# Transformer layer on one core: the last products taken in another tile order, one balancing loop of fifty steps, and the final mixing shared by four engines

## The reference

```python
x = x + xattn(layernorm(x), ctx, mask, ...)      # 32 heads, 256 context rows
x = x + attn(layernorm(x), Wq, Wk, Wv, Wo)       # causal, rotary, 32 heads of 32
x = x + ffn(layernorm(x), ...)

def ffn(x, ...):                 # x in 4 streams of 256 columns
    x_norm = x * rsqrt(mean(x * x) + eps)
    H_res = sinkhorn_log(x_norm @ W_res.T + H_res_base)      # 4 x 4 a row
    H_pre = softmax(x_norm @ W_pre.T + H_pre_base)
    H_post = softmax(x_norm @ W_post.T + H_post_base)
    H_res = (1 - g) * I + g * H_res
    y = einsum('btnc,btn->btc', x_streams, H_pre) @ W_branch
    return einsum('btij,btjc->btic', H_res, x_streams) + einsum('btc,btn->btnc', y, H_post)
```

## Time and profile before

| | |
|---|---|
| median of 3 runs | 1153.63 us (1153.41 to 1156.05) |
| profiled execution, its own time | 1153.41 us |
| its span, first to last instruction | 1151.6 us |
| mean granted TensorE clock | 0.978 of full |
| busy, PE / DVE / ACT / POOL | 93% / 70% / 41% / 13% |
| chain that ended last, by engine | PE 82%, DVE 14%, ACT 2% |

### The profile page before, as it was taken

How to read it: one execution, slowest core, us unless ns; L and a number is a source line. 1 busy time by engine, 2 the same in 40 slices (tenths; PEclk the granted TensorE clock), 3 DMA queues, 4 the chain that set the end, 5 groups by cost and what they waited for, 6 DMA issues and landing times.

```text
span 1151.6 us, 17668 instructions
## 1 busy us (share of the span) xinstructions
PE 1071.5 (93%) x6392; PEld 899.6 (78%) x6392; DVE 808.7 (70%) x1843; ACT 477.0 (41%) x989; POOL 154.7 (13%) x162
## 2 busy tenths in 40 slices
PE   5999999999999999999999999999999999895565
PEld 3888888888888887888888887888888778784444
DVE  6744447567768868776678876675547799836998
ACT  4523324354454446544544455432223334313334
POOL 0000000333223222332332220000001000000000
PEclk9999999999999999999999999999999999997778
DMA  9876757243443233344334312899835322000001
GB/s 236 189 163 144 159 124 168 55 101 89 102 105 73 68 73 69 75 98 101 93 90 104 70 33 61 172 218 245 172 74 109 57 42 35 14 2 1 0 1 73
DMA packets 163803, 111.12 MB, mean 96 GB/s; under 512 B 73224, under 2 KB 155784, under 8 KB 163744
## 3 DMA queue, kind: packets, MB, share of 16 engines
q1 hardware_dynamic: 161488, 109.24, 43.3%
q10 hardware_dynamic: 2256, 1.11, 0.4%
HBM read 90.91 MB, written 18.87 MB: 95 GB/s over the span
## 4 chain that ended last, share of the span: by engine, by line
PE 82%; DVE 14%; ACT 2%; issue 1%; DMA 1%; POOL 0%; ACTq 0%; DVEq 0%
PE ps L533 29%; PE ps L476 28%; PE ps L864 8%; PE ps L462 5%; PE ps L544 4%; PE ps L561 4%; DVE wt L1381 1%; DVE xr L2023 1%; DVE small L1906 1%; DVE small L1930 1%; DVE small L1910 1%; DVE small L1903 1%; DVE small L1927 1%; DVE small L1921 1%; PE ps L650 1%
## 5 line engine op out<-in xcount | busy, mean ns | idle before, releaser
L533 PE MATMUL ps<-wt,act 128*128 128x512 f32 x1536 | 389.1, 396 | 0.0
L476 PE MATMUL ps<-wt,act 128*128 128x512 f32 x1440 | 330.1, 391 | 4.0 <-DVE wt L1381 3.9
L476 PEld LDWEIGHTS ps<-wt,act 128*128 128x128 f32 x1440 | 271.1, 189 | 60.8 <-DVE act L1365 4.3
L533 PEld LDWEIGHTS ps<-wt,act 128*128 128x128 f32 x1536 | 275.9, 188 | 49.5
L1381 DVE TENSOR_TENSOR wt<-raw,wt 128x512 fp32r<-128x512 f32 x192 | 120.0, 682 | 84.9 <-ACT wt L967 84.9
L967 ACT ACTIVATE wt<-raw 128x512 fp32r<-128x512 f32 x192 | 106.5, 623 | 94.5 <-PE ps L476 52.7
L1365 DVE TENSOR_TENSOR act<-ps,act 128x512 fp32r<-128x512 f32 x112 | 75.9, 683 | 78.4 <-ACT act L962 78.4
L1373 DVE STREAM_TRANSPOSE raw<-raw 128x1024 f32<-128x1024 f32 x92 | 108.0, 1217 | 31.4 <-DMA raw<-in_L_xattn_o_proj_w 20.7
L864 PE MATMUL ps<-wt,act 128*128 128x512 f32 x480 | 121.0, 400 | 1.7 <-issue 1.0
L962 ACT ACTIVATE act<-ps 128x512 fp32r<-128x512 f32 x112 | 65.9, 596 | 114.2 <-PE ps L462 113.9
L2036 POOL TENSOR_TENSOR small<-small 128x4 f32<-128x4 f32 (+2 forms) x64 | 70.8, 1109 | 278.5 <-DVE small L1395 213.7
(11 more groups left out here) (145 smaller groups left out, 1086.4 us busy)
## 6 DMA issues: line engine op xcount, KB each, us to landing
xr<-in_ctx SPq DMA_DIRECT2D x64, 256.0 KB, 5.7
raw<-in_L_xattn_o_proj_w SPq DMA_DIRECT2D x32, 512.0 KB, 13.9
raw<-in_L_xattn_q_proj_w SPq DMA_DIRECT2D x28, 512.0 KB, 9.6
q_rows<-G SPq DMA_DIRECT2D x64, 128.0 KB, 3.5
xr<-q_rows SPq DMA_DIRECT2D x16, 512.0 KB
ot_hi<-spare SPq DMA_DIRECT2D x64, 128.0 KB, 2.6
act<-ot_hi SPq DMA_DIRECT2D x32, 256.0 KB, 9.0
raw<-in_L_xattn_k_proj_w SPq DMA_DIRECT2D x8, 512.0 KB, 9.0
```

The source lines that it names most:

```text
L476: mm = pe.matmul(banks[t], lhs(p == 2, c, t), wt[:, n_slot, int(p == 1), c, :], start=(acc_from and q == 0), stop=(acc_to and q == 3 * NC ...
L533: mm = pe.matmul(bank, src[int(p == 2)][:, c, kt * P:(kt + 1) * P], wt[:, slot, int(p == 1), c, :], start=(q == 0), stop=(q == 3 * NC - 1))
```

## The change

Order of the last products: steps 8 to 15 go by `LAST`, that is tiles 0 and 1 with both units, then tiles 2 and 3 with both. So the residual of tiles 0 and 1 is final earlier, and unit 24 must be split by step 10: its chunks are taken 4 and 4 in steps 9 and 10. The transposes and logits move with them (`TURNED` gives the count of the wait of each); the transposes of the 24 rows come a step earlier. Logits 2 and the first half of logits 3 stand inside the last step.

Balancing: chain 0 runs 1 + 3 + 3 + 1 iterations (`LEAD`) between the last additions. Then both chains run together up to chain 0's 50th, with no part where one runs alone; the folding at iteration 25 takes three multiplications (`fold_outer`, `fold_root` twice), with the square root of the exponentials that ScalarE makes at the start, in the place of logarithms and new exponentials. Chain 0's finish is woven into an iteration of chain 1, which then runs 7 more.

Mixing: tile 0 as before. Tile 1: ScalarE scales streams of `z` into `share` (16 instructions of 128 x 256) and GpSimd adds them to `xr`, 8 additions of 128 x 512. Tiles 2 and 3: streams 0 and 1 by diagonals and TensorE, streams 2 and 3 by VectorE, 16 instructions in place of 32. The stores go by the order in the diff, six of them.

```diff
...
 ROW = 4
 NSTR, CW = 4, 256
-ITERS, EPOCH, HEAD = 50, 25, 4
+ITERS, EPOCH = 50, 25
+LEAD = (1, 3, 3, 1)
+LAST = ((0, 0), (1, 0), (0, 1), (1, 1), (2, 0), (3, 0), (2, 1), (3, 1))
+TURNED = {(0, 0): (1, 0), (0, 1): (2, 0), (1, 0): (3, 1), (1, 1): (4, 2),
+          (2, 0): (5, 3), (3, 0): (6, 5), (2, 1): (7, 4), (3, 1): (8, 7)}
...
+        share = [raw1[:, 2048 + 512 * k:2560 + 512 * k] for k in range(4)]
...
+        late_base = ps[:, 6:8, 256:512]
         kacc = [ps[:, 2, :], ps[:, 3, :]]
         vacc = [ps[:, 6, :], ps[:, 7, :]]
...
                 sp.dma_start(w24[a:a + n, :], w).then_inc(w24_loaded, 16)
-            for t, half, signal, count in ((0, None, mix_out, 2), (2, None, out_ready, 1), (1, None, mix_out, 4),
-                                           (3, 0, out_ready, 2), (3, 1, out_ready, 3)):
+            for t, half, signal, count in ((0, None, mix_out, 2), (1, None, pool_mixed, 8), (2, 1, out_ready, 1),
+                                           (2, 0, mix_out, 3), (3, 1, out_ready, 2), (3, 0, mix_out, 4)):
                 sp.wait_ge(signal, count)
...
+                for half, bank in enumerate(open_banks[t]):
                     for i in (2 * half, 2 * half + 1):
                         for j in range(NSTR):
-                            pe.wait_ge(d_res, 16 * t + 4 * i + j + 1)
-                            mm = pe.matmul(bank[:, (i % 2) * CW:(i % 2 + 1) * CW], dres[t][:, 4 * i + j, :],
+                            pe.wait_ge(d_res, ready + 4 * i + j + 1)
+                            mm = pe.matmul(bank[:, (i % 2) * CW:(i % 2 + 1) * CW], dres[t % 2][:, 4 * i + j, :],
                                            z[:, t, j * CW:(j + 1) * CW], start=False, stop=(i % 2 == 1 and j == NSTR - 1))
                     mm.then_inc(mix_done, 1)
...
+                if b >= 8:
+                    t, n = LAST[b - 8][0], 23 + LAST[b - 8][1]
...
-                    elif b >= 12:
-                        if b >= 13:
-                            turn_rows(b - 13, 1)
-                        turn_rows(b - 12, 0)
+                    elif b == 11:
+                        turn_rows(0, 0)
+                        turn_rows(0, 1)
+                    elif b == 12:
+                        logits(0)
+                        turn_rows(1, 0)
+                        turn_rows(1, 1)
+                    elif b == 13:
+                        turn_rows(2, 0)
+                    elif b == 14:
+                        turn_rows(3, 0)
+                    elif b == 15:
+                        turn_rows(2, 1)
 
...
+                    if b == 15:
+                        logits(2)
+                        logits(3, 0, 4)
...
-                if b == 11:
+                if b == 10:
                     pe.wait_ge(w24_loaded, 64)
...
-                if b == 12:
...
-                if b >= 13:
-                    logits(b - 13)
+                if b == 12:
+                    logits(1)
...
-            logits(3)
+            logits(3, 4, NC)
...
-            for t in range(2):
+            for t in (0, 2, 3):
                 mix(t)
...
-                     6: (23, (4, 5)), 7: (23, (6, 7)), 9: (24, (0, 1)), 10: (24, (2, 3, 4)), 11: (24, (5, 6, 7))}
+                     6: (23, (4, 5)), 7: (23, (6, 7)), 9: (24, (0, 1, 2, 3)), 10: (24, (4, 5, 6, 7))}
...
+                sc.wait_ge(sk_in[c], 1)
+                answer(c, Kx)
+                sc.wait_ge(sk_in[c], 2)
+                answer(c, Kx)
+                sc.wait_ge(sk_out[c], 2)
+                answer(c, A, 0.5)
...
+                if t == 1:
+                    sc.wait_ge(base_done, t + 1)
+                    sc.activation(xr[:, t, :].rearrange("p (h n) -> p h n", h=2), ps[:, 2:4, :], ACT.Copy).then_inc(base_added, 1)
                 if t >= 2:
                     sc.wait_ge(base_done, t + 1)
-                    for half in range(2):
-                        a = sc.activation(xr[:, t, half * UW:(half + 1) * UW], ps[:, base_banks[t][half], :], ACT.Copy)
-                    a.then_inc(base_added, 1)
+                    sc.activation(xr[:, t, UW:E].rearrange("p (i n) -> p i n", i=2), late_base, ACT.Copy
+                                  ).then_inc(base_added, 1)
...
-            branch(0)
-            branch(1)
-            log_chain(0)
-            exp_chain(0)
-            log_chain(1)
-            exp_chain(1)
-            branch(2)
-            branch(3)
-            for t in range(2):
-                sc.wait_ge(h_ready, 1)
-                for n in range(16):
-                    sc.activation(dres[t][:, n, :], ident[:], ACT.Copy, scale=hres[:, 16 * t + n:16 * t + n + 1]
+            for t in range(NT):
+                branch(t)
+
...
+
+            def mixed(t, half):
+                k = half if t == 0 else t
+                sc.wait_ge(mix_done, k + 1)
+                sc.activation(xr[:, t, half * UW:(half + 1) * UW], open_banks[t][half], ACT.Copy).then_inc(mix_out, 1)
+
+            def scale_rows(half):
+
+                for j in range(NSTR):
+                    if half:
+                        sc.wait_ge(pool_mixed, j + 1)
+                    for i in range(2):
+                        c = 16 + 4 * (2 * half + i) + j
+                        a = sc.activation(share[j][:, i * CW:(i + 1) * CW], z[:, 1, j * CW:(j + 1) * CW], ACT.Copy,
+                                          scale=hres[:, c:c + 1])
+                    a.then_inc(scaled, 1)
+
+            sc.wait_ge(base_done, 4)
+            diagonals(0, 0, 8)
+            scale_rows(0)
+            diagonals(0, 8, 16)
+            scale_rows(1)
+            mixed(0, 0)
+            mixed(0, 1)
+            diagonals(2, 0, 8)
+            diagonals(3, 0, 8)
+            mixed(2, 0)
+            mixed(3, 0)
...
                 else:
-                    add_tile(68 + b, b - 9, 0, acc2)
-                    first_stats3(b - 9)
+                    add_last(0, 1)
...
+            def fold_outer(c):
+
+                stepped(c)
+                rows = two(ua[c]).unsqueeze(3).broadcast_to([P, 2, NSTR, NSTR])
+                step(c, v.tensor_tensor(rows4(of(tk, c)), rows, over_i(ub[c]), ALU.mult))
+
+            def fold_root(c, dst):
+                answered(c, 3)
+                stepped(c)
+                step(c, v.tensor_tensor(of(dst, c), of(tk, c), of(A, c), ALU.mult))
...
+            def iterate(chains):
+
+                fold = [c for c in chains if iterated[c] == EPOCH]
                 for c in chains:
-                    stepped(c)
-                    step(c, v.tensor_tensor(rows3(of(tk, c)), rows3(of(Kx, c)), over_j(ua[c]), ALU.mult))
+                    iterated[c] += 1
+                    if c in fold:
+                        fold_outer(c)
+                    else:
+                        scale_cols(c)
+                for c in fold:
+                    fold_root(c, tk)
+                    fold_root(c, Kx)
                 for c in chains:
-                    stepped(c)
-                    step(c, v.tensor_reduce(two(ub[c]), cols4(of(tk, c)), AX, ALU.add))
-
-            def invert_cols(c, last=False):
+                    sum_rows(c, Kx if c in fold else tk)
...
-            last_stats3(0)
-            last_stats3(1)
+            add_last(1, 1)
             logits(0)
-            last_stats3(2)
+            add_last(2, 0)
             logits(1)
             centre_rows(0)
             centre_cols(0)
-            last_stats3(3)
             first_iteration3(0)
+            for _ in range(LEAD[0]):
+                iterate((0,))
+            add_last(3, 0)
+            for _ in range(LEAD[1]):
+                iterate((0,))
+            add_last(2, 1)
+            for _ in range(LEAD[2]):
+                iterate((0,))
             logits(2)
-            for _ in range(HEAD):
+            add_last(3, 1)
+            for _ in range(LEAD[3]):
                 iterate((0,))
             logits(3)
...
-            joint = EPOCH - 1 - HEAD
-            for k in range(joint):
-                iterate((0, 1), last=0 if k == joint - 1 else None)
+            for k in range(ITERS - iterated[0]):
+                iterate((0, 1))
...
-            for k in range(HEAD):
-                if k == HEAD // 2:
-                    recentre(0)
-                iterate((1,), last=1 if k == HEAD - 1 else None)
-            for k in range(HEAD):
-                if k == HEAD // 2:
-                    recentre(1)
-                iterate((0,), fresh=0 if k == 0 else None)
-            for k in range(ITERS - EPOCH - HEAD):
-                iterate((0, 1), fresh=1 if k == 0 else None)
-            finish(0)
-            for k in range(HEAD):
+            iterated[1] += 1
+            finish_cols(0)
+            scale_cols(1)
+            finish_gate(0)
+            sum_rows(1, tk)
+            finish_diagonal(0)
+            invert_rows(1)
+            scale_rows(1)
+            sum_cols(1)
+            invert_cols(1)
+            for _ in range(ITERS - iterated[1]):
```

(33 more changed lines are left out.)

210 lines of the change are left out of this document (106 added, 104 removed).

## The result

The changed kernel takes 1150.57 us (median of 8 runs, 1149.08 to 1151.89), the kernel before in the same series 1154.29 (8 runs). The ratio is 0.9966, with a 95% interval of 0.9954 to 0.9977: 3.7 us faster, where 9.6 were forecast. The time lies above the range of 1141 to 1149. The profiled execution took 1151.28 us with a span of 1149.4 (before 1153.41 and 1151.6); forecast were 1144.0 and 1142.2. So 7.2 us have to be found.

The account below looks back on a forecast made before the run. TensorE bounds until about 1050 us, then VectorE's dependent iterations. Chain 1's numbers at 1128.4, ScalarE ready 1129.6, TensorE from 1130.0 plus 6.9 and 1.75, copy 0.7, store 2.8: span 1142.2, time 1144.0 us; range 1141 to 1149.

Parts of the forecast that it names:

- Part 1: Up to the logits: low-part wait +1.26 us, last step's extra logits +2.55, logits 3 on VectorE at 1055.0.
- the 1.2 us expected from the logits: Last logits reach VectorE at 1055.0, 1.2 us before the 1056.21 of the kernel before.
- Part 2: Balancing on VectorE: 41 joint iterations at 1.389 us, softmax 0.52, folding 0.92; chain 0's finish starts at 1116.5.
- The step that failed: VectorE's eight iterations of chain 1 after chain 0, the first with chain 0's finish woven in: 11.1 us.
- the rule against it: Trainium skill: GpSimd contends with VectorE instructions having two SBUF inputs, as two of six iteration steps do; forecast took nothing.
- The sign that the prediction had named: Listed as showing the forecast wrong: a VectorE iteration of 1.6 us or more beside GpSimd's additions.
- GpSimd holds VectorE up: Rival: GpSimd's 10.3 us of additions delay chain 1; half or less lost, 1148.0 (12%), about all, 1153.1 (3%).
- the slower rival: GpSimd's additions take twice as long and VectorE stands still for them, 20.6 us: 1163.4 us; chance 3%.
- Part 3: Mixing: VectorE's additions 6.95 us, ScalarE's sixteen scaled copies 6.5, TensorE's last passes at low clock; span ends at 1142.2.
- The start at low clock: TensorE's last 32 passes begin at half clock after a 3.5 us pause, costing 1.75 us over 6.9.

Follow-up runs that it names:

- Lo_first: Changed kernel with the low part of the attention's output taken before the four weight chunks in step 9 of VectorE's loop; 1146.71 us, ratio 0.9947.
- warm_front: Changed kernel with twenty unused transposes in TensorE's wait of 2.50 us for the low part of step 9; 1149.81 us, ratio 0.9968.
- before_chunks: Kernel before the change, with only the change's four weight chunks of unit 24 in step 9 and four in step 10; 1154.99 us, ratio 1.0015.
- short_adds: Changed kernel with GpSimd's eight additions cut to 8 of 512 columns, the rest of tile 1's mixing left out; 1144.54 us, ratio 0.9922.
- Runs 1 and 2: Run 1 is short_adds. Run 2: changed kernel, chain 1's matrix copied to PSUM so its multiplications read one SBUF tile; 1144.52 us, ratio 0.9921.
- 3 and 4: Changed kernel. Run 3: each GpSimd addition made as two of 256 columns, 1144.84 us. Run 4: GpSimd copies 512 columns instead of adding, 1144.42 us.

## Why the prediction was wrong

**Part 1** held in its mechanism: a wait of 2.50 for the low part, additions and iterations that interleave with no wait for VectorE but one of 0.78 behind the last addition, for which the sum had 0.8. Missing was the clock behind the wait, 2.3 us. The logits 3 stand at 1056.43 where 1055.0 was forecast, the joint start at 1059.26 where it was 1058.1 (and 1059.34 before); this execution reached the place 0.86 earlier than the profiled one before, which hides part of the loss and is luck. So the 1.2 us expected from the logits are gone. Lo_first confirms the place (chain 0's finish 4.0 earlier); warm_front, before_chunks and short_adds show that the clock's share isn't the same in every run.

**Part 2** up to chain 0's finish: 1059.26 to 1117.90 is 58.64, forecast 58.4. Right, the folding included.

**The step that failed** is the one on the eight iterations of chain 1 alone. They were priced at 11.1 us, and the rule against it was set aside "because 32 columns are a small part of a step of 0.23". Measured: 17.32. The size of VectorE's step has nothing to do with it: a step with two inputs in SBUF ends only when the running GpSimd addition has ended, so a step of 0.19 becomes one of 0.91. Runs 1 and 2 show the cause from two sides, 3 and 4 the law. The sign that the prediction had named, an iteration of 1.6 or more beside GpSimd's additions, is in the trace: 2.8 where both multiplications are held. The rival "GpSimd holds VectorE up" is the one that came true, with 6.0 of 10.3 us lost, between its two cases (half, 12%, 1148.0; about all, 3%, 1153.1). It priced the loss as a share of GpSimd's time and had no rule for the share. By the prediction's own sum this step alone gives 1149.0, the upper end of its range; the lateness of the front and the longer burst put the time beyond it. The rule is a count: each of the 8 additions catches one of the two multiplications of an iteration, and an idle stretch of two short steps is all that remains between. What the slower rival had against it, that GpSimd would "have to stop steps of 32 columns for whole additions", is what happens, but GpSimd itself does not slow (1.27 each, forecast 1.29), so the loss stays under one addition for each. The rule of the Trainium skill that was weighed ("GPSIMD Engine Reference", section "Key points": contention where VectorE has two SBUF inputs) agrees with the trace: 0.19 against 0.91.

The prediction also says that nothing in the trace of before shows both engines with two inputs from SBUF. There are such places, GpSimd and then VectorE:

```profile
1033.46 1.06 POOL L2036 TENSOR_TENSOR small<-small 128x1 f32<-128x1 f32 x2 [6.84 <-DVE small L1820]
...
1033.68 0.24 DVE L1833 SCALAR_TENSOR_TENSOR small<-G,small 128x24 f32<-128x24 f32 x1
```

L2036 raises one column to powers given in another, L1833 reads two tiles of 24 columns, and it is not held: it takes 0.24 as it does alone at 1056.4. The splits of 128 x 512 (L1381) took 0.68 to 0.70 beside such instructions, 0.68 alone. So these rows would have pointed the wrong way. Every GpSimd instruction that held VectorE in the runs moved 256 or 512 columns; those of 1 to 8 columns held nothing, even where they lasted a microsecond. Where between 8 and 256 columns it begins, no run shows.

**Part 3**: scaled copies 3.29 for eight, 0.40 to 0.41 each (0.407 forecast, between bounds of 0.2925 and 0.502). ScalarE was ready at 1130.88 (1129.6 forecast, 1.3 late as all else). VectorE's sixteen additions took 6.80 (6.95 forecast). The start at low clock was priced at 1.75; the burst took 9.94 where 8.65 was forecast, at 0.50 from 1136 to 1142 (the term of 1.75 was thus 3.0; the clock had been at 0.50 since 1132, in a pause of 7.23 where 3.5 was forecast):

```profile
1136.00:1142.00 6.00, 5.55 (x13) 4.47 (x14) 5.89 (x15) 4.79 (x16) 0.00 (x0) 0.50 0.00 0
```

**The sum of the miss.** Chain 1's numbers come 7.6 late (1135.99 against 1128.4: 1.4 from the front, 6.2 from the eight iterations and the finish), less 1.2 in which ScalarE would not have been ready: 6.4. The burst adds 1.3, and the last copy and store together take 0.5 less than priced: 7.2. The prediction's sum has two slips of its own, both small: ScalarE's line adds up to 1129.5, not 1129.6, and the 0.2 from the profiled execution to the median was named and not added (1144.2).

What stays open: why the clock falls at one of two stops in one run and at the other in the next, and why the second burst takes 7.17 in three of the kernels, 8.7 to 8.9 in six, 9.94 in the changed one and 10.08 in warm_front. The length of the pause in front doesn't order them: in lo_first it was 7.99, and the burst took 8.69.

## What to carry to other kernels

Before giving GpSimd elementwise work beside a dependent chain on VectorE, count the chain's steps that read two tiles of SBUF, and its multiplications by a scalar: each can be held until a GpSimd instruction of hundreds of columns ends, however small the step is. Put one operand in PSUM, or cut GpSimd's instructions short. And when a change adds a wait in front of TensorE, price its length and the stretch at half clock that may follow: here 1.3 and up to 2.3 us.
